# Sixteen places for gated rows, table entries sixteen at a time, and six images' rows read back during the tile loop

## The reference

```python
x = x + conv_block(group_norm(x), ...)      # 3x3 depthwise, batch norm, relu, 1x1, batch norm, relu
t = to_tokens(x)                            # (image, 784 tokens, 128 channels)
t = t + attention(layer_norm(t), Wq, Wk, Wv)
flat = layer_norm(t).reshape(-1, 128)
logits = flat @ Wr                          # 8 experts
top_vals, top_idx = top_k(logits, 2)
top_w = softmax(top_vals)
for e in range(8):
    hdn = gelu(flat @ W1[e] + b1[e])        # 128 -> 512
    y = hdn @ W2[e] + b2[e]                 # 512 -> 128
    out = out + gates[:, e:e + 1] * y       # gates: top_w where e was chosen, else 0
t = t + out
x = from_tokens(t)
```

## Time and profile before

| What | Value |
|---|---|
| Median of 3 runs | 873.25 us (873.24 to 874.97) |
| The profiled execution's own time | 869.77 us |
| Its span | 868.0 us |
| PE busy, matmuls | 718.1 us (83%) |
| DVE busy | 593.9 us (68%) |
| POOL busy | 499.3 us (58%) |
| ACT busy | 470.5 us (54%) |
| Moved by DMA | 86.52 MB, mean 100 GB/s |

### The profile page before, as it was taken

How to read it: one execution, slowest core, us unless ns; L and a number is a source line. 1 busy time by engine, 2 the same in 40 slices (tenths; PEclk the granted TensorE clock), 3 DMA queues, 4 the chain that set the end, 5 groups by cost and what they waited for, 6 DMA issues and landing times. The chain is left out here.

```text
span 868.0 us, 20320 instructions
## 1 busy us (share of the span) xinstructions
PE 718.1 (83%) x6460; PEld 556.1 (64%) x6460; DVE 593.9 (68%) x1793; ACT 470.5 (54%) x922; POOL 499.3 (58%) x501
## 2 busy tenths in 40 slices
PE   0689989999999999799589967669999999994433
PEld 0355656666666666566368957658999999994322
DVE  3657888888878888877757646545666666663666
ACT  1235546676655655465458746446777777772000
POOL 4100057777777776666556777777677666775000
PEclk9999999999999999999679988889999999998555
DMA  8601102222233222122164333336664544442997
GB/s 243 125 19 57 56 26 89 90 91 89 90 95 95 94 93 66 33 71 73 49 108 82 83 75 66 78 72 128 105 99 92 97 91 94 82 89 68 281 310 242
DMA packets 123038, 86.52 MB, mean 100 GB/s; under 512 B 96484, under 2 KB 105192, under 8 KB 122947
## 3 DMA queue, kind: packets, MB, share of 16 engines
q1 hardware_dynamic: 106034, 52.86, 26.5%
q0 software_dynamic: 13888, 26.03, 11.0%
q10 hardware_dynamic: 3024, 6.43, 2.0%
HBM read 30.50 MB, written 35.48 MB: 76 GB/s over the span
## 5 line engine op out<-in xcount | busy, mean ns | idle before, releaser
L473 POOL DMA_INDIRECT dispatched_rows<-rows,pos x224 | 215.3, 961 | 96.3 <-issue 66.3
L484 POOL DMA_INDIRECT expert_rows<-xb_x,dest x210 | 217.8, 1037 | 90.9 <-issue 67.9
L738 PE MATMUL pair_d<-w,xb_x 128*128 x2520 | 177.2, 222 | 0.1
L532 PE MATMUL pair_a<-padx,tap_diag 128*128 128x392 f16 x864 | 162.9, 335 | 0.0
L738 PEld LDWEIGHTS pair_d<-w,xb_x 128*128 128x128 f16 x2520 | 158.2, 99 | 5.0 <-issue 0.2
L912 ACT ACTIVATE xb_x<-seen_g 128x512 f16<-128x512 f32 x210 | 120.9, 624 | 67.7 <-PE pair_d L738 64.0
L1328 DVE TENSOR_TENSOR xb_x<-seen_g,xb_x 128x512 f16<-128x512 f32 x210 | 135.7, 687 | 17.5 <-ACT xb_x L912 17.1
L532 PEld LDWEIGHTS pair_a<-padx,tap_diag 128*128 128x128 f16 x864 | 83.1, 99 | 58.2 <-issue 3.9
L1346 DVE TENSOR_TENSOR xb_x<-pair_d,share 128x256 f32<-128x256 f32 x105 | 44.5, 424 | 93.1 <-PE pair_d L738 67.1
L721 PE MATMUL pair_b<-xrt,w 128*128 128x256 f16 x636 | 80.6, 278 | 2.3 <-DMA xrt<-dispatched_rows 2.3
L721 PE MATMUL pair_c<-xrt,w 128*128 128x256 f16 x624 | 79.1, 278 | 0.0
(11 more groups left out here) (211 smaller groups left out, 1148.3 us busy)
## 6 DMA issues: line engine op xcount, KB each, us to landing
xb_x<-in_x SPq DMA_DIRECT2D x32, 392.0 KB, 4.0
w<-expert_rows SPq DMA_DIRECT2D x16, 784.0 KB, 6.6
t_all<-t SPq DMA_DIRECT2D x16, 392.0 KB, 2.9
out<-w ACTq DMA_DIRECT2D x16, 392.0 KB, 5.6
t_all<-in_L_ffn_W SPq DMA_DIRECT2D x16, 256.0 KB, 6.2
dispatched_rows<-rows,pos POOLq DMA_INDIRECT x224
expert_rows<-xb_x,dest POOLq DMA_INDIRECT x210
dispatched_rows<-pad_rows SPq DMA_DIRECT2D x16, 131.0 KB
```

Of the source, the lines that this page charges most:

```text
L473: pool.indirect_dma_start(xs, bass.IndirectOffsetOnAxis(ap=pos[:, u, t, k:k + 1].bitcast(U32), axis=0), rows[:, u, t, :].bitcast(U32), Non ...
L484: pool.indirect_dma_start(ys, bass.IndirectOffsetOnAxis(ap=dest[:, half, slot, s:s + 1].bitcast(U32), axis=0), y[:, slot, s, :], None, bou ...
L532: last = T.matmul(pa[:, h * BANK:h * BANK + HALF], tap_diag[:, wp, tap, :], padx[:, xp, u, ky + 14 * h:ky + 14 * h + 14, kx:kx + SIDE], st ...
L738: last = T.matmul(dst, ghl[:, t % 2, gp, f * TILE + s * P:f * TILE + (s + 1) * P], w2[:, wp, bass.ds(w0 + f * P, P)], start=False, stop=(f ...
```

## The change

1. **Stores.** The gated rows `y` get sixteen places (`STORE_DEEP`) and the destinations `dest` four batches (`STORE_BATCHES`). The semaphores `stored_0` to `stored_3` now count by batch of four tiles. `gated` no longer waits for a store; `fields` of batch `q` waits for the stores of batch `q-4`.
2. **PE's table entries** come sixteen at a time (`TAKE`), seven loads for 27.
3. **Late tiles by age.** `late_tables` lists, behind the 72 early tiles, first every expert's tiles that hold rows of the first 13 images, then the rest. So all rows of those images lie in the first 88 tiles (`KNOWN`). The tables get twice the runs (16 for 8) and a second count.
4. **Reading back early.** In SP's queue, behind the load of tile 94, stands a wait for the stores of the first 88 tiles, and behind the loads of tiles 94, 96, ... 104 one read of an image's rows each, images 0 to 5. There are eight places for read-back rows (`ROW_BUFFERS`), six of them in `p1_area`, the memory of tensors that only the first stage uses, two where `yl` was. The other ten images are read when all stores have landed, each as soon as the sum of the image eight before has been made.
5. **Memory.** First-stage tensors are put together in `p1_area` and `conv_y`; `y` lies in `conv_y`. POOL sets two more constants at the start and a larger `upto`. The loop over pairs in the last stage is written out on SP and DVE.

```diff
+KNOWN = -(-((2 * EARLY_IMAGES * L + E * (TILE - 1)) // TILE + 1) // DEEP) * DEEP
+FETCHED, ROW_BUFFERS = 6, 8
+FETCH_AT = tuple(range(94, 94 + 2 * FETCHED, 2))
+STORE_BATCHES = 4
+TAKE = 16
+STORE_DEEP = STORE_BATCHES * DEEP
...
-        y = xb_x1[:, 2 * FC * TILE:2 * FC * TILE + DEEP * 2 * P].rearrange("p (u s c) -> p u s c", u=DEEP, s=2)
+        y = conv_y[:, 0:STORE_DEEP * 2 * P].rearrange("p (u s c) -> p u s c", u=STORE_DEEP, s=2)
...
+        fetched = p1_area[0:TT, :].rearrange("p (u t k d) -> p u t k d", u=FETCHED, t=NT, k=2)
+        later = w1_place[0:TT, 0:(ROW_BUFFERS - FETCHED) * 2 * NT * P].rearrange("p (u t k d) -> p u t k d", u=ROW_BUFFERS - FETCHED, t=NT, k=2)
...
+        def store_uses(b, tiles=TILES):
+            return sum(1 for t in range(tiles) if t // DEEP % STORE_BATCHES == b)
...
+            def load_y(i):
+
+                if some(i + 1 - ROW_BUFFERS):
+                    sp.wait_ge(S["ysum_ready"], i + 1 - ROW_BUFFERS)
+                sp.dma_start(rows_of(i).rearrange("p t k d -> p (t k d)"), y_img[i]).then_inc(S[f"yl_loaded_{i % ROW_BUFFERS}"], 16)
...
                 load_tile(t)
+                if t == FETCH_AT[0]:
+                    for b in range(STORE_BATCHES):
+                        sp.wait_ge(S[f"stored_{b}"], 32 * store_uses(b, KNOWN))
+                if t in FETCH_AT:
+                    load_y(FETCH_AT.index(t))
+
+
+            for b in range(STORE_BATCHES):
+                sp.wait_ge(S[f"stored_{b}"], 32 * store_uses(b))
+            for i in range(FETCHED, IMAGES):
+                load_y(i)
...
+            const(G.memset(region_step[:], float(REGION)))
...
-            take_experts(0, 2)
+            take_experts(0, TAKE)
             hidden(0)
-            take_experts(2, DEEP)
...
-                if t % DEEP == DEEP - 1 and t + 3 < TILES:
-                    take_experts(t + 3, min(DEEP, TILES - t - 3))
+                if (t + 3) % TAKE == 0 and t + 3 < TILES:
+                    take_experts(t + 3, min(TAKE, TILES - t - 3))
...
+                counts(link, early_base[:, :], 0, ALU.is_gt, late[:, 0, E:2 * E])
+                V.tensor_copy(late[:, 1, 0:E], late[:, 0, E:2 * E])
+                counts(link, base[:, :], 0, ALU.is_gt, late[:, 1, E:2 * E])
...
+                tile_table(link, late[:, 4, 0:2 * E], late[:, 3, 0:2 * E], EARLY, LATE, tsmall[:, 8, 0:1], 2 * E)
...
-                if some(32 * (q - 1)):
-                    for slot in range(DEEP):
-                        dve.wait_ge(S[f"stored_{slot}"], 32 * (q - 1))
+                place, uses = q % STORE_BATCHES, q // STORE_BATCHES
+                if some(uses):
+                    dve.wait_ge(S[f"stored_{place}"], 32 * DEEP * uses)
...
-                if some(32 * q):
-                    dve.wait_ge(S[f"stored_{slot}"], 32 * q)
```

More of the change, by code:

```diff
@@ L66 @@
 PADS_AT = 44
-POOL_CONSTS = 28
+POOL_CONSTS = 30
 W_LOADS = 17
@@ L140, in build, with part @@
         shift = sb("shift", [P, NORMS], F32)
[L141 to L146 removed]
+        p1_area = sb("p1_area", [P, FETCHED * 2 * NT * P], F32)
+        taken = [0]
+        def part(words):
+            taken[0] += words
+            assert taken[0] <= FETCHED * 2 * NT * P, taken
+            return p1_area[:, taken[0] - words:taken[0]]
+        xn = part(NT * P)[0:TT, :].rearrange("p (t c) -> p t c", t=NT)
+        xt = part(L)
+        xf = part(NT * P)[0:TT, :].rearrange("p (t c) -> p t c", t=NT)
+        sq = part(L // 2).bitcast(BF16)
+        sk = part(L // 2).bitcast(BF16)
+        sv = part(NT * P // 2)[0:TT, :].bitcast(BF16)
         seen_g = sb("seen_g", [P, NT * (L + TT)], BF16)
         seen = seen_g[0:TT, :]
[L149 removed]
+        t2 = part(2 * L).rearrange("p (u l) -> p u l", u=2)
         t2_all = sb("t2_all", [P, IMAGES * L], F32)
         staged = t2_all[:, IMAGES * L - 2 * E * HID:IMAGES * L].rearrange("p (n e h) -> p n e h", n=2, e=E)
[L152 removed]
+        rows = part(NT * ROW)[0:TT, :].bitcast(F16).rearrange("p (u t c) -> p u t c", u=2, t=NT)
         pos = sb("pos", [TT, 2, NT, 2], I32)
[L154 removed]
+        rt = part(12 * NT * E)[0:TT, :].rearrange("p (k n) -> p k n", k=12)
+        tap_diag = part(TAPS * P).bitcast(F16).rearrange("p (n t c) -> p n t c", n=2, t=TAPS)
+        w_raw = part(4 * P).rearrange("p (n c) -> p n c", n=4)
+        b2_raw = part(E * P)[0:1, :]
         rs = sb("rs", [TT, 12, NT], F32)
@@ L165, in build @@
         over = tbig[:, 1, 0:E * MAXT].rearrange("p (e m) -> p e m", e=E)
-        upto = sb("upto", [P, E, E], F32)
+        upto = sb("upto", [P, 2 * E, 2 * E], F32)
+        region_step = sb("region_step", [P, 2 * E], F32)
+        late = sb("late", [P, 5, 2 * E + 1], F32)
         early_base = sb("early_base", [P, E], F32)
@@ L212, in build, with rows_of @@
             "dest_ready", "y_ready", "y_copied", "stored_0", "stored_1", "stored_2", "stored_3",
-            "yl_loaded_0", "yl_loaded_1", "ysum_ready", "yt_ready", "o_ready", "out_0", "out_1",
+            "yl_loaded_0", "yl_loaded_1", "yl_loaded_2", "yl_loaded_3", "yl_loaded_4", "yl_loaded_5", "yl_loaded_6", "yl_loaded_7", "ysum_ready", "yt_ready", "o_ready", "out_0", "out_1",
         )}
+        def rows_of(i):
+            b = i % ROW_BUFFERS
+            return fetched[:, b] if b < FETCHED else later[:, b - FETCHED]
         block = ctx.enter_context(nc.Block())
@@ L1237, in body, with counts @@
                     early_tables()
-            def counts(link, from_, shift_, compare, n):
+            def counts(link, from_, shift_, compare, into):
                 link(V.scalar_tensor_tensor(out=tsmall[:, 0, :], in0=descend[:, :], scalar=float(REGION), in1=from_, op0=ALU.mult, op1=ALU.add))
@@ L1243, in counts, with summed, tile_table @@
                 link(V.tensor_tensor(over, bc_last(tsmall[:, 1, :], MAXT), tcount[:, :, :], compare))
-                link(V.tensor_reduce(tsmall[:, n, :], over, AX.X, ALU.add))
-            def summed(link, n, into):
-                sums = tbig[:, 0, 0:E * E].rearrange("p (a b) -> p a b", a=E)
-                link(V.tensor_tensor(sums, upto[:, :, :], bc_mid(tsmall[:, n, :], E), ALU.mult))
-                link(V.tensor_reduce(tsmall[:, into, :], sums, AX.X, ALU.add))
-            def tile_table(link, ends, skips, t0, count, first):
-                ended = tbig[:, 0, 0:count * E].rearrange("p (t e) -> p t e", e=E)
-                skipped = tbig[:, 1, 0:count * E].rearrange("p (t e) -> p t e", e=E)
-                link(V.tensor_tensor(ended, bc_last(tile_no[:, 0:count], E), bc_mid(ends, count), ALU.is_ge))
+                link(V.tensor_reduce(into, over, AX.X, ALU.add))
+            def summed(link, numbers, into, n):
+                sums = tbig[:, 0, 0:n * n].rearrange("p (a b) -> p a b", a=n)
+                link(V.tensor_tensor(sums, upto[:, 0:n, 0:n], bc_mid(numbers, n), ALU.mult))
+                link(V.tensor_reduce(into, sums, AX.X, ALU.add))
+            def tile_table(link, ends, skips, t0, count, first, runs):
+                ended = tbig[:, 0, 0:count * runs].rearrange("p (t e) -> p t e", e=runs)
+                skipped = tbig[:, 1, 0:count * runs].rearrange("p (t e) -> p t e", e=runs)
+                link(V.tensor_tensor(ended, bc_last(tile_no[:, 0:count], runs), bc_mid(ends, count), ALU.is_ge))
                 V.tensor_reduce(tile_expert[:, t0:t0 + count], ended, AX.X, ALU.add)
@@ L1400, in _ @@
             add_rows(1, 0, 1)
-            with dve.Fori(1, PAIRS) as j:
+            for j in range(1, PAIRS):
                 sum_rows(2 * j, j, 0)
```

79 lines of the change are left out of this document (29 added, 50 removed).

## The result

The changed kernel takes **861.77 us** in the median of four executions (860.92 to 862.48), the kernel before 874.11 us beside it: the ratio is 0.9858, 95% interval 0.9841 to 0.9875. It is 1.4% faster. The forecast was 849.8 us with a range of 840 to 862, so the time lies inside the range by 0.2 us. The profiled execution took 860.92 us, with a span of 859.2 us.

A forecast was written before the change was run, and what follows sets the result against it. POOL was taken to bound until 618 us, PE to 797, DMA bytes in the last stage. An earlier loop end and fewer late bytes saved 24.0 us, 23.4 after the start: span 844.6, median 849.8 us, range 840 to 862.

The forecast's parts named there:

- Start, +0.6: At the kernel's start, POOL's larger constants delay PE's first work: 0.6 us added, with nothing to cover it.
- POOL's price, 2.72 us a tile: In the tile loop, a saturated POOL needs 2.72 us a tile, 45 tiles from tile 42 taking 122.4 us.
- the 3.58 us of that rival: Tile loop: DVE's `split` meets every store, raising POOL's price to 3.58 us a tile; median 902 us, chance 4%.
- Sixteen places, -1.1 at tile 28: Tile loop to tile 42: POOL's wait for DVE at 536.77 us mostly goes, -1.1 us, between 0 and -1.7.
- SP's wait at tile 94, dry for 1.4 us: Late tile loop: PE stops 15 to 20 us, POOL's tiles in hand nearly hide it; dry 1.4 us, bounds 0 and 20.
- Late tables, 0: At tile 26, extra table instructions cost DVE 4 to 5 us, covered by POOL's lag of 20 us: 0.
- PE's entries, 0: Tile loop: 20 fewer loads of entries save PE 10 us only if PE were the bound; worth 0 by itself.
- The last stage is a matter of bytes, 53.3 us behind the last store: Last stage: DMA bytes set the time, 13.2 MB at 305 GB/s taking 43.4 us, then 7.5 us after the last read.
- reads crowd out the writes: Last stage rival: queued reads delay writes, DVE has two places `o`, a pair stays at 7.8 us; median 858, chance 14%.
- DVE bounds: Last stage rival: DVE, at 5.95 us a pair, sets the pace instead of DMA; median 843 us, chance 12%.
- everything else idles: Last stage before the change, from 802 us: DMA engines 0.91 busy at 278 GB/s, all other engines idle.
- 305 GB/s at a full share: Last stage: full DMA engines move these rows at 305 GB/s, rather than the skill's 425 GB/s.

The follow-up runs named there:

- run 1: The changed kernel without its early reads and SP's wait in the tile loop, all 16 images read after all stores landed: 869.7 us, ratio 0.9977.
- run 6: The kernel before the change with one more table of POOL's constants at its start, so PE starts later: ratio 1.0019, in a job with slower times.
- run 9: The changed kernel with SP's wait behind the load of tile 95 instead of 94, and reads but the last one tile later: 852.03 us, ratio 0.9778.
- runs 5 and 11: The changed kernel with PE taking four table entries at a time instead of sixteen, timed twice in jobs with slower times: ratios 0.9907 and 0.9904.
- Run 4: The changed kernel with four places for finished images (o) instead of two: 847.81 us, ratio 0.9731.
- Run 10: The changed kernel with thirteen images read early, all behind tile 104's loads, and four places for finished images (o): 827.65 us, ratio 0.9491.

## Why the prediction was right or wrong

**Right in sign and kind, 12 us too low in the time.** Of the gain of 23.4 us that was forecast 12.3 came. From the last store's landing to the end the kernel saved 13.5 us (56.6 for 70.1) of 16.8 reckoned, but the loop ended 4.7 us later than before, not 6.6 sooner. That 861.77 still lies under the high end of 862 is luck in part. That end was made for crowded writes and a later restart, which both came; but some 4 us were lost ahead of the tiles, where the forecast had no term, and in the last stage two errors cancelled.

*Start, +0.6.* PE's first work is at 11.50 us, +0.46. Right.

*POOL's price, 2.72 us a tile.* From tile 43 to 88 it took 123.4 us, 2.74 a tile (run 1: 2.76). Right, and with it the verdict that POOL bounds the loop. It is 2.55 us where DVE stands (tiles 84 to 90), 2.76 where it runs. The Trainium skill (SBUF — State Buffer, Who interferes with whom) says that a DVE instruction with two SBUF inputs contends with a GpSimd instruction that reads SBUF, and not with one that only writes it, which the prediction left out. The trace has that sign, 0.2 us a tile, far from the 3.58 us of that rival; no run changes DVE's instructions to show that this is the cause.

*Sixteen places, -1.1 at tile 28.* Wrong: tile 0 to 28 took 127.5 us for 126.0 before, and 126.4 to 128.8 in the runs under usual conditions. The wait at 536.77 us went, but POOL's 84 DMAs took 2.2 us more (91.15 us for 88.91), mostly the 28 row DMAs (1.08 us each for 1.02). Whether a DVE that no longer stops lengthens them was not tested. That is 2.6 us of the 7.3 up to tile 88.

*Before the tiles.* Tile 0 was stored at 455.86 us for 451.64: 3.8 us beyond the start. No term had this. It varies by as much between executions, as run 6's section shows, and is the largest part of the 7.3; that none of it is the change's is not shown.

*SP's wait at tile 94, dry for 1.4 us.* **This is the step that failed.** The length of the stall was right (18.6 us for 15 to 20), and "PE has rows to tile 94" was too, though PE stood for DVE and not for rows. But "POOL has tiles 88 to 92 in hand" looked at PE's queue alone. `fields` works in batches of four, and in DVE's order gates 91 and on stand behind the fields of tile 95. POOL was dry at 755.5 us, with steps of 5.3, 3.3 and 3.5 us at tiles 91 to 93 and another of 5.4 at 99. The wait with its reads cost 8.4 us by run 1, of which run 9 took away 7.6. The forecast allowed 3.6 in all (its 49.8 us between the landings, less 17 tiles at 2.72), so it was 4 to 5 us short, and that is the miss of 4.0 between the landings.

*Late tables, 0.* The trace agrees: from 540 us to tile 88 POOL has no pause for DVE over the fixed 0.30 us.

*PE's entries, 0.* Not contradicted; not shown either (runs 5 and 11).

*The last stage is a matter of bytes, 53.3 us behind the last store.* It took 56.6, close, for the wrong reason in part: bytes and writes in the way to 839 us, DVE's 5.55 us a pair behind. The rival "reads crowd out the writes" (858 us) had the mechanism (two places `o`, writes up to 9.95 us), and "DVE bounds" the pace of the second half (5.55, reckoned 5.95). Run 4 prices the first at 9.8 us. Without it the stage takes 46.0 us behind the last store (798.76 to 844.8), 7 less than forecast, since the bytes go faster than 305 GB/s there (363 and 372 in its windows of 10 us from 807 to 827 us). These are the two errors that cancelled. That "everything else idles" in this stage before the change was too strong: the earlier trace rows has DVE busy for 42.01 of 66 us.

*305 GB/s at a full share.* Run 10 moved 379 GB/s at a share of 1.02. So 305 was the rate of that mix, not a limit. The Trainium skill (DMA: Bandwidth & Descriptors, Bandwidth) gives 425 GB/s for a 16 MB load; no window shown here reached it, and 379 is nearer to it than to 305.

## What to carry to other kernels

When an in-order queue is made to wait, list everything behind the wait for every engine, down to the smallest load, and count in the batches in which it is used. Here tile 95's rows and its 3 KB of fields went ahead of the wait, and the reads one tile later, and nearly its whole cost was gone. A transfer that becomes slow does harm only through the places that it holds, so look first for the place with the fewest copies. And where one engine is behind by 20 us, faster partners gain nothing until work is found that needs only what has already been stored.
